# Six more tiles above the diagonal are kept for sweep 1 of a two-layer graph network

## The reference

```python
def _L0_gnn_ref(values, adjacency, W, b):
    fc_sc = values @ W + b
    d_inv_sqrt = 1.0 / (jnp.sqrt(jnp.sum(adjacency, axis=1)) + 1e-08)
    laplacian = adjacency * d_inv_sqrt[:, None] * d_inv_sqrt[None, :]
    return laplacian @ fc_sc

def _L1_gnn_ref(X, adj, W, b):
    adj_hat = adj + jnp.eye(adj.shape[0], dtype=adj.dtype)
    d_inv_sqrt = 1.0 / jnp.sqrt(jnp.sum(adj_hat, axis=1))
    adj_norm = adj_hat * d_inv_sqrt[:, None] * d_inv_sqrt[None, :]
    return jax.nn.relu(adj_norm @ (X @ W) + b)

x = _layernorm(x + _L0_gnn_ref(x, adj, L0_gnn_W, L0_gnn_b), axis=-1)
x = _layernorm(x + _L1_gnn_ref(x, adj, L1_gnn_W, L1_gnn_b), axis=-1)
```

## Time and profile before

| | |
|---|---|
| median of 3 runs | 1849.18 us (1848.67 to 1849.58) |
| profiled execution, its own time | 1849.2 us |
| span of its trace | 1847.3 us |
| PE busy | 1659.9 us, 90% |
| DVE busy | 1208.0 us, 65% |
| ACT busy | 755.1 us, 41% |
| POOL busy | 161.6 us, 9% |
| DMA | 573.38 MB, 310 GB/s over the span |
| granted TensorE clock, mean | 0.962 |

### The profile page before, as it was taken

How to read it: one execution, slowest core, us unless ns; L and a number is a source line. 1 busy time by engine, 2 the same in 40 slices (tenths; PEclk the granted TensorE clock), 3 DMA queues, 4 the chain that set the end, 5 groups by cost and what they waited for, 6 DMA issues and landing times.

```text
span 1847.3 us, 16886 instructions
## 1 busy us (share of the span) xinstructions
PE 1659.9 (90%) x6136; PEld 1123.5 (61%) x6136; DVE 1208.0 (65%) x1550; ACT 755.1 (41%) x904; POOL 161.6 (9%) x177
## 2 busy tenths in 40 slices
PE   0357899999999999978899999999999999999996
PEld 0123344444444444446777777877877878888885
DVE  1344556776866685347756656455465999999996
ACT  5544333111000000034544444444444777777774
POOL 0000000000000000011100000000000011111111
PEclk9768899999999999989999999999999999999998
DMA  9999999998888766246676665666565999999992
GB/s 386 421 421 421 421 421 402 397 401 343 363 338 359 315 248 265 104 157 239 224 258 225 227 242 200 222 227 225 204 228 215 419 419 412 393 387 388 395 398 84
DMA packets 85906, 573.38 MB, mean 310 GB/s; under 512 B 10400, under 2 KB 10656, under 8 KB 20288
## 3 DMA queue, kind: packets, MB, share of 16 engines
q1 hardware_dynamic: 76320, 541.23, 74.1%
q0 software_dynamic: 9504, 31.07, 4.3%
HBM read 556.79 MB, written 15.47 MB: 310 GB/s over the span
## 4 chain that ended last, share of the span: by engine, by line
PE 74%; DVE 12%; DMA 9%; issue 2%; ACT 1%; POOL 1%; SPq 0%; DVEq 0%; ACTq 0%
PE acc L675 30%; PE acc L699 14%; PE acc L701 14%; PE acc L700 14%; DMA lent<-adj_tiles 5%; DVE low L818 5%; DMA own<-adj_tiles 2%; DMA own<-adj_far 1%; DMA lent<-adj_far 1%; DVE stats L796 1%; PE turned L611 1%; DVE run L829 1%; DVE h L894 1%; PE mixed L642 1%; PE acc L689 1%
## 5 line engine op out<-in xcount | busy, mean ns | idle before, releaser
L699 PE MATMUL acc<-high,feat_high 128*128 128x512 f32 x1336 | 535.1, 401 | 40.9 <-DVE low L818 31.8
L675 PE MATMUL acc<-lent,feat 128*128 128x512 f32 x1168 | 533.9, 617 | 19.9 <-DVE feat L866 14.7
L701 PE MATMUL acc<-high,feat_low 128*128 128x512 f32 x1336 | 526.7, 394 | 0.0
L700 PE MATMUL acc<-low,feat_high 128*128 128x512 f32 x1336 | 526.2, 394 | 0.0
L818 DVE TENSOR_TENSOR low<-own,high 128x1024 fp32r<-128x1024 f32 x330 | 391.3, 1221 | 183.3 <-ACT high L718 180.5
L718 ACT CAST high<-own 128x1024 fp32r<-128x1024 f32 x330 | 339.0, 1055 | 208.8 <-PE acc L701 196.0
L675 PEld LDWEIGHTS acc<-lent,feat 128*128 128x128 f32 x1168 | 230.0, 198 | 310.6 <-issue 293.8
L829 DVE TENSOR_TENSOR run<-run,lent 128x2048 f32<-128x2048 f32 x135 | 309.4, 2292 | 132.8 <-DMA lent<-adj_tiles 127.7
L699 PEld LDWEIGHTS acc<-high,feat_high 128*128 128x128 f32 x1336 | 254.4, 190 | 101.4 <-issue 44.8
L701 PEld LDWEIGHTS acc<-high,feat_low 128*128 128x128 f32 x1336 | 254.5, 190 | 55.3
L700 PEld LDWEIGHTS acc<-low,feat_high 128*128 128x128 f32 x1336 | 254.9, 191 | 50.8
(11 more groups left out here) (69 smaller groups left out, 674.1 us busy)
## 6 DMA issues: line engine op xcount, KB each, us to landing
lent<-adj_tiles SPq DMA_DIRECT2D x237, 1024.0 KB, 11.6
own<-adj_tiles SPq DMA_DIRECT2D x197, 1024.0 KB, 6.0
lent<-adj_far SPq DMA_DIRECT2D x60, 1024.0 KB, 22.1
own<-adj_far SPq DMA_DIRECT2D x18, 1024.0 KB, 23.0
x_in<-x_rows POOLq DMA_DIRECT2D x32, 256.0 KB, 6.4
sums_rows<-stage POOLq DMA_DIRECT2D x27, 256.0 KB, 6.6
sums_in<-sums_rows POOLq DMA_DIRECT2D x27, 256.0 KB, 8.8
x_t<-x_cols SPq DMA_DIRECT2D x16, 256.0 KB, 14.7
```

The source lines that it names most:

```text
L675: mm = nc.tensor.matmul(bank, feat0[:, j * Q + q, :], raw(n)[:, q * T:(q + 1) * T], start=(u == plan.first[g] and q == 0), stop=(u == plan ...
L699: nc.tensor.matmul(bank, f_high, a_high[:, chunk], start=(u == plan.first[g] and q == 0), stop=False)
L700: nc.tensor.matmul(bank, f_high, a_low[:, chunk], start=False, stop=False)
L701: mm = nc.tensor.matmul(bank, f_low, a_high[:, chunk], start=False, stop=(u == plan.last[g] and q == Q - 1))
```

## The change

Only the list `NEAR` changes:

```diff
-NEAR = [3] * NB
+NEAR = [3] * 4 + [4] * 3 + [3] * 7 + [4, 5]
```

## The result

| | before | after |
|---|---|---|
| median, runs on the same chip | 1848.67 us (1847.07 to 1849.58) | 1856.01 us (1855.24 to 1859.54) |
| ratio, 95% interval | | 1.005 (1.0039 to 1.0061) |
| profiled execution, its own time | 1849.2 us | 1855.4 us |
| span of its trace | 1847.3 us | 1853.6 us |

The account below looks back on a forecast made before the run. PE was taken as the bound, except DMA up to about 340 us and row chains from 810 to 893 us. Terms +23.2, +3.4, -10 and -8.2 make +8.4 on 1849.2: 1858 us, range 1843.6 to 1868.4 (own range 1852 to 1864).

Parts of the forecast that it names:

- part 4: Rows 0 to 2 in sweep 2: three layer-0 products fewer in PE's stretch, -8.2 us (bounds -8.2 to -6).
- part 1: Rows 4 to 7, DMA stage: held tiles leave fewer turning slots, so loads wait for takes, +23.2 us (13 to 28).
- 12.5 + 3.44 (k-1): Rows 4 to 7: us from a row's last landing to the end of take k after the degree, when slots come free.
- Part 2: Row 15 of sweep 1: one more take, (10,14), where PE is never idle, +3.4 us (bounds 3.4 to 5).
- Part 3: Seam of the sweeps: two more takes, three products fewer, shorter PE waits, -10 us net (bounds -1.3 and -14).
- A: Rival, rows 4 to 7: the queue stays fed and the loads are hidden, so faster, 1836 us; chance 0.12.
- C: Rival, rows 4 to 7: PE idles too little to restart slowly, slot cost 13 us, 1848 us; chance 0.12.
- B: Rival, seam of the sweeps: stalls only move, so -1.3 us instead of -10, 1867 us; chance 0.14.
- D: Rival: the edit does nothing, as tiles are held but their products stay in sweep 2; excluded beforehand, no chance of its own.
- Exchange: Later rival, anywhere: a held tile costs 3.44 us in sweep 1, returns 2.72 in sweep 2, slots irrelevant; no chance given.

Follow-up runs that it names:

- the low column: Column 4 alone raised from three held tiles to four, by adding (0,4), against the kernel before: 1851.71 us, ratio 1.0026.
- the low columns: Columns 4, 5 and 6 alone raised from three held tiles to four, against the kernel before: 1864.63 us, ratio 1.0091.
- the slots: Kernel before with takes and products unchanged, but three slots kept out of use until columns 4, 5 and 6 are taken: 1868.19 us, ratio 1.0112.
- the high tiles alone: Columns 14 and 15 alone raised from three held tiles to four and five, against the kernel before: 1841.15 us, ratio 0.9957.
- the best one: Against the kernel before, columns 8 to 10 hold one tile, column 11 two, column 15 four, the others three: 1822.83 us, ratio 0.9869.
- the one a step further: Columns 7 and 11 hold two tiles, 8 to 10 one, 15 four, the others three, against the kernel before: 1826.62 us, ratio 0.9889.

## Why the prediction was right

The forecast was +8.8 us on the median, 1858 with a range of 1843 to 1869; measured were +7.3 and 1856.0. That the sum is this near is partly luck: part 4 gave 5.2 us more than forecast, by a clock that the forecast had not priced, and made up for 1.2 us more in part 1 and 1.6 us of slow restarts of PE in row 8. By its steps:

**Part 1, the slots: right, +24.4 against +23.2.** Forecast row lengths 43.1, 47.6, 49.1, 50.0; measured 43.7, 49.3, 48.8, 49.2. The gated loads were issued at 241.72 (k = 6 after 211.92 gives 241.6), 286.86 (k = 5 after 261.26: 287.6) and 338.59 (k = 6 after 310.07: 339.8), so the rule "12.5 + 3.44 (k-1)" held within 1.2 us. These loads landed 4.9, 4.7 and 5.1 us after their issue, where the forecast had 4.8. The estimate by the Trainium skill (DMA: Bandwidth & Descriptors, the anatomy of one DMA), 4.4 us, is below all three; that section is on DMAs that GpSimd issues, and these are SP's. Two things were left out. In each of rows 5 to 7 a second gate follows, after take 7 (in row 5 the loads at 245.15 and 245.53), and the chain goes through it. It is not shown to cost time: in row 5 the DMA share was 1.01 from 244 us on, before that gate opened, so the DMA engines were at full rate in the 1.7 us by which that row is longer than forecast, and what they moved in them is open. And PE restarts more slowly in row 8, since it has idled longer before it (3.57 us against 2.35): +0.8. The holes came where they were named: the share stood at 0.10 or less for 6, 7 and 4 us in rows 5, 6 and 7 (forecast: 6 to 8). The run with three slots fewer shows that the cause is the slots, not only that the place is right.

**Part 2, (10,14): right, +4.2 against +3.4,** of which 0.8 is the half-clock start in row 8, that is 43.85 us for 96 matmul records against 43.01. No landing in rows 11 to 15 showed.

**Part 3, the seam: right in size (-10.1 against -10) by luck, wrong in its make-up.** The forecast took nearly all of it from PE's waits. The first take of sweep 2 came 7.9 us later relative to the column of 15 (7.6 forecast). But the sum of the idle time fell only from 26.8 to 23.4 us in the stretch between degree 15 and row 9 (139.40 - 112.58 against 129.30 - 105.87). The other 6.7 us are busy time, and the work there shrank by only 1.3. So some 5.4 us were saved because fewer matmuls ran at 1.2 GHz: the mean clock there is 0.93 where it was 0.90, and 15 matmuls of sweep 2 last longer than 0.6 us there instead of 40 (25 x 0.20 = 5.0 us). This comes with the high tiles: the five traces without them (the kernel before twice, the low column, the low columns, the slots) have 38 to 41 such matmuls there, the kernels with one, two and three high tiles 23, 18 and 18. The waits of the changed kernel there:

```profile
PE acc L699 <- DVE feat_low L910: 11.1, 2, 5.9
PE acc L699 <- DVE low L818: 6.3, 7, 1.8
```

Waits for low parts, 10.1 us before in this stretch, went down as forecast; the wait before the first take of sweep 2 grew from 3.38 us to 5.91 us (the forecast let the turns fill that time), and a second wait for features, 5.20 us, follows at 862.22. And the three tiles aren't equal, which the prediction, pricing them in one sum, could not see. With (11,15) alone the waits are these:

```profile
PE acc L699 <- DVE low L818: 6.4, 6, 1.8
PE acc L699 <- DVE feat_low L910: 6.0, 2, 3.6
```

And the first take of sweep 2, in the changed kernel and with (11,15) alone:

```profile
847.60 0.76 PE L699 MATMUL acc<-high,feat_high 128*128 128x512 f32 x1 [5.91 <-DVE feat_low L910]
...
810.19 0.76 PE L699 MATMUL acc<-high,feat_high 128*128 128x512 f32 x1 [2.44 <-issue]
```

The low parts gain the same, and the waits for features stay at 6.0 us in all (5.7 before). Nearly all of the seam's gain comes with the one tile that completes row 11 in sweep 1: -8.2, against -9.4 with all three high tiles and nothing else. The long waits for features (5.9 and 5.2 us) come only with (10,15): with (11,15) and (10,14) they are 6.0 us in all. Why row 11 gives the gain is read from the waits; no run tests it apart.

**Part 4, rows 0 to 2 in sweep 2: mis-sized, -13.4 against -8.2.** The work is as forecast, and PE's waits for low parts from row 9 on are no shorter (19.8 us in the stretch below of the changed kernel, 19.4 in that of the kernel before). What the step lacked is the clock. Busy time of sweep 2 without the seam, before and after:

```profile
893.00:1438.00 545.00, 525.59 (x2351) 430.81 (x2350) 312.70 (x445) 249.73 (x287) 36.45 (x50) 0.99 0.63 228
```

```profile
914.00:1443.00 529.00, 509.22 (x2302) 417.00 (x2301) 310.65 (x440) 245.75 (x280) 37.96 (x49) 1.00 0.64 236
```

(The two stretches aren't cut at the same landmarks: 2.6 of the 16.0 us between them lie at their ends, and 13.4 are the step's.) The forecast had taken 0.99 as good as 1.00. TensorE's timeline of the kernel before, row 8:

```profile
953.53 0.47 PE L699 MATMUL acc<-high,feat_high 128*128 128x512 f32 x1 [1.81 <-DVE low L818]
...
954.53 0.39 PE L700 MATMUL acc<-low,feat_high 128*128 128x512 f32 x1
954.75 0.57 PE L701 MATMUL acc<-high,feat_low 128*128 128x512 f32 x1
955.12 0.63 PE L699 MATMUL acc<-high,feat_high 128*128 128x512 f32 x1
955.55 0.63 PE L700 MATMUL acc<-low,feat_high 128*128 128x512 f32 x1
```

After an idle 1.81 us and 1.6 us of work the matmuls start 0.43 us apart instead of 0.23, seven of them. There are four such stretches in the kernel before (at 955.1, 996.1, 1211.2 and 1279.1 us, 28 slow matmuls), each after a wait of 1.81 us for a low part at a row chain. 28 x 0.20 = 5.6 us, about the 5.2 that the step missed. In the changed kernel the same place of row 8 has an idle time of 1.79 us and full speed:

```profile
973.17 0.47 PE L699 MATMUL acc<-high,feat_high 128*128 128x512 f32 x1 [1.79 <-DVE low L818]
...
975.55 0.39 PE L700 MATMUL acc<-low,feat_high 128*128 128x512 f32 x1
```

It has none of these stretches. The two halves bear this out: from degree 15 to the end of sweep 2 the kernel before has 68 matmuls longer than 0.6 us, the low columns alone 54, the high tiles alone 44 and the whole change 15. The halves lose 38 of them and the whole 53, so the halves should add up to 15 x 0.20 = 3.0 us more than the whole; they add up to 3.2 more. The change doesn't remove the waits that precede the stretches, so this gain is no merit of fewer products. Whether it belongs to the list or to the execution is not shown, with one profile of the changed kernel.

**The rivals.** *A, hidden loads* (1836) and *C, half the cost* (1848) fall with the row lengths and with the low columns alone. By the double-buffering rule of the Trainium skill (Trainium Kernel Development and Optimization, Best Practices), as the prediction cites it, A was the outcome; here six or seven turning slots weren't enough, and three fewer with nothing else changed cost 20.6 us. *B, a seam that gives nothing* (1867) falls with -10.1 us in the trace and -6.5 us for the high tiles alone. *D* falls with the work. *Exchange*, the later rival, falls with the same two runs.

**What stays open:** whether a wait of 1.8 us is followed by a half-clock stretch or not. Waits of the same length in the same trace went either way: of the nine of 1.81 us in the kernel before, four were followed by one. But over all 14 traces, from row 9's chain to the end of sweep 2, 25 of the 64 such waits of 1.80 to 1.82 us were followed by a stretch, and 1 of the 36 of 1.74 to 1.79 us. The length of the wait and the stretches go together, then. No run changed such a wait alone, so neither its length nor its place in time is shown as the cause.

## What to carry to other kernels

A buffer held for longer is paid in the stage that reads fastest: count which load waits for which product, add the landing time and the loads queued behind it, and compare that round with the time the bytes need. Price each item of a bundled change alone, since here three items cost 17.0 us and the other three gave 6.5, nearly all of it by one of them. Read the clock of each stage beside its waits: two of the four terms of this forecast gained some 5 us each from it, unpriced. A stage where the bound engine is never idle is where work can be moved out, up to the point where it waits again.

## What the runs showed of the hardware

- **One waiting load empties the queue for all behind it.** With nine turning slots a mean share of 1.01 was held between 150 and 340 us; with six or seven it stood at 0.10 or less for 4 to 7 us in each of rows 5 to 7, though TensorE was working all the while. In row 5 nothing was issued for 10.3 us. After the issue at 241.72 the share was back at 1.01 by 244 us, and the load itself had landed 4.9 us after its issue.
- **Half-clock stretches inside a dense stream.** Granted clock 0.50 for seven matmuls (0.63 us instead of 0.39), about 1.4 us lost each time, after an idle time of only 1.8 us. A second profiled execution of the kernel before (29 slow matmuls) had them at 953.5, 994.5, 1148.1 and 1278.0 us: three of the four places again, one elsewhere. The places at 955 and 996 us recur, as far as the seam is shifted, in all five traces whose columns 8 to 15 are those of the kernel before. Other lists of `NEAR`, with one profile each, had none from row 9 on (the changed kernel, the one tile, columns 8 to 13 at two, the best one and the one a step further) up to four (the high tiles). So the places depend on the schedule, and on the execution in part. A full set is some 6 us, nearly the spread of the kernel before over the 16 runs whose median is 1847.62 (1843.43 to 1850.58). A change of one take (3.4 us) can be read from the row lengths of the trace, hardly from the total.
